# 35 expert tiles a layer in place of 36, and the score banks of each layer's first batch exchanged

## The reference, cut to what matters

```python
x = x + cross_attention(layernorm(x), ctx_1024)        # once, 16 batches of 112 rows of 256
y = layernorm(x)
for l in range(4):                                     # four layers
    y = clip(y + attention(rms(y, ln1_w[l]), wq[l], wk[l], wv[l], wo[l]), -100, 100)
    h = rms(y, ln2_w[l])
    probs = softmax(h @ wr[l]); the two best of 8 experts, their weights made to sum to 1
    y = clip(y + sum over the two experts e of weight * ((silu(h @ wg[l,e]) * (h @ wu[l,e])) @ wd[l,e]), -100, 100)
return x + y
```

## Time and profile before

| | |
|---|---|
| median of 3 runs | 2210.82 us (2205.89 to 2211.4) |
| the profiled execution | 2209.43 us |
| its span, first to last instruction | 2207.6 us |
| mean granted TensorE clock | 0.978 |
| instructions recorded | 34643 |

### The profile page before, as it was taken

The page is one execution under the profiler, slowest core; times in us unless marked ns, Lnnn a source line. Parts: engine busy times, 40 slices in busy tenths (PEclk is TensorE's granted clock), DMA queues, the critical chain, the costliest instruction groups (busy, mean ns, idle before and its releaser), DMA issues.

```text
span 2207.6 us, 34643 instructions
## 1 busy us (share of the span) xinstructions
PE 2062.9 (93%) x9889; PEld 1525.7 (69%) x9890; DVE 1330.2 (60%) x2960; ACT 1033.7 (47%) x3743; POOL 523.4 (24%) x624
## 2 busy tenths in 40 slices
PE   5768999989999999989999999989999999999994
PEld 4646788766667888766667888766667887766663
DVE  4645887764335788754345887744346778844345
ACT  2211667653333766653333667643334676542331
POOL 2212232243012223143011222232011322322023
PEclk9979999999999999999999999999999999999997
DMA  6610233022121232023121222022121331022123
GB/s 187 182 29 34 74 99 103 1 79 84 45 57 52 74 126 71 2 79 89 43 63 44 99 99 70 33 66 76 45 65 35 103 127 39 14 82 69 46 70 94
DMA packets 92023, 157.41 MB, mean 71 GB/s; under 512 B 13874, under 2 KB 65668, under 8 KB 91780
## 3 DMA queue, kind: packets, MB, share of 16 engines
q1 hardware_dynamic: 75988, 114.12, 16.2%
q0 software_dynamic: 15904, 41.64, 6.6%
HBM read 108.75 MB, written 46.97 MB: 71 GB/s over the span
## 4 chain that ended last, share of the span: by engine, by line
PE 62%; DVE 19%; ACT 9%; issue 4%; POOL 3%; DMA 1%; DVEq 0%; SPq 0%; POOLq 0%; ACTq 0%
PE ps L808 23%; PE ps L827 11%; ACT parena L1092 8%; DVE rope L1426 6%; PE ps L707 5%; PE ps L779 5%; PE ps L817 3%; PE ps L728 3%; PE ps L715 2%; PE ps L743 2%; POOL qk L520 2%; DVE rmax L1436 2%; PE ps L682 2%; DVE qk L1414 2%; PE ps L802 1%
## 5 line engine op out<-in xcount | busy, mean ns | idle before, releaser
L808 PE MATMUL ps<-arena,xeT 128*128 x1152 | 544.4, 595 | 5.8 <-ACT xeT L1130 4.5
L1092 ACT ACTIVATE parena<-ps,nmax 112x112 f32<-112x112 f32 x1024 | 345.5, 388 | 120.0 <-DVE nmax L1437 120.0
L808 PEld LDWEIGHTS ps<-arena,xeT 128*128 128x128 f32 x1152 | 209.2, 192 | 151.9 <-issue 144.8
L520 POOL TENSOR_TENSOR qk<-qk,rope 128x448 f32<-128x448 f32 x128 | 148.8, 1163 | 668.0 <-DVE rope L1426 667.8
L1140 ACT ACTIVATE parena<-ps,er 128x512 f32<-128x512 f32 x144 | 99.0, 687 | 405.6 <-PE ps L808 402.0
L707 PE MATMUL ps<-xnT,wqk_s 128*128 128x224 f32 x1280 | 275.7, 359 | 8.9 <-ACT parena L1092 8.0
L487 POOL DMA_INDIRECT y_in<-sorted_y,pos x150 | 143.8, 959 | 554.9 <-DMA sorted_y<-tarena 427.3
L827 PE MATMUL ps<-arena,tarena 128*128 x1152 | 272.6, 379 | 0.8 <-ACT tarena L1146 0.8
L1092 ACT ACTIVATION_READ_ACCUMULATOR parena<-ps,nmax 112x1 f32 x1024 | 246.5, 241 | 0.0
L707 PEld LDWEIGHTS ps<-xnT,wqk_s 128*128 128x128 f32 x1280 | 234.7, 193 | 14.2 <-ACT parena L1092 11.4
L728 PE MATMUL ps<-qk 128*112 128x224 f32 x1024 | 239.5, 356 | 0.0
(11 more groups left out here) (186 smaller groups left out, 2767.6 us busy)
## 6 DMA issues: line engine op xcount, KB each, us to landing
xe<-sorted_x SPq DMA_DIRECT2D x144, 130.0 KB, 2.1
sorted_y<-tarena SPq DMA_DIRECT2D x144, 128.0 KB
arena<-in_L_ffn_wg_dram SPq DMA_DIRECT2D x32, 512.0 KB, 3.6
arena<-in_L_ffn_wu_dram SPq DMA_DIRECT2D x32, 512.0 KB, 4.5
arena<-in_L_ffn_wd_dram SPq DMA_DIRECT2D x32, 512.0 KB, 5.5
arena<-in_ctx_dram SPq DMA_DIRECT2D x16, 375.0 KB
sorted_x<-tarena POOLq DMA_DIRECT2D x8, 585.0 KB, 6.0
sorted_y<-tarena POOLq DMA_DIRECT2D x8, 576.0 KB, 4.9
```

Of the source, the lines that this page charges most:

```text
L520: pool.tensor_tensor(q, q, rope[m % 2][:, :], ALU.add).then_inc(g_rope, 1)
L808: last = pe.matmul(ps[:, bank, :], xeT[u][:, k, :], w[:, bass.ds(e * 1024 + k * 512, 512)], start=(k == 0), stop=(k == KD - 1))
L1092: last = act.activation(prob[:, n, :], ps[0:S, bank, h * S:h * S + S], ACT.Exp, bias=nmax[:, b % 2, n:n + 1], scale=SCALE, accum_out=rsum[ ...
```

## The change

NT becomes 35. TILES holds how many tiles each of the two buffers takes: 18 even and 17 odd. The last tile, 34, is now an even one and uses banks 0 and 1, so batch 0 of each layer has its score halves exchanged: p = 0 in banks 2 and 3, p = 1 in banks 0 and 1 (`score_bank`), and the heads computed during batch 0 move from banks 1 and 2 to 2 and 3. AHEAD stays 26, so that the written out tiles are 26 to 34 in place of 26 to 35. Waits are renumbered to fit. The core of the diff:

```diff
-NT = B * S * TOPK // SLOT + E
+NT = B * S * TOPK // SLOT + E - 1
+TILES = ((NT + 1) // 2, NT // 2)
...
-        ZP = 96
-        zero = tarena[0:ZP, 0:6 * DX].rearrange("p (r d) -> p r d", r=6)
-        rows = ZP * 6
+        ZP = 112
+        zero = tarena[0:ZP, 0:5 * DX].rearrange("p (r d) -> p r d", r=5)
+        rows = ZP * 5
...
-        def heads(p):
+        def score_bank(b, p):
+            return 2 * p if b else 2 - 2 * p
+        def heads(b, p):
+            n = score_bank(b, p)
...
                 with sp.Fori(WHOLE // 2 - 1, NT // 2 - 1) as i:
                     pair(i)
-                if last:
-                    store_rows(0)
-                pair(NT // 2 - 1, end=True)
-                store_tile(NT - 1, 1)
+                load_tile(NT - 1, 0)
+                for T in range(NT - 4, NT):
+                    store_tile(T, T % 2)
+                    if last and T == NT - 3:
+                        store_rows(0)
...
                     if b:
-                        if odd and more:
+                        if odd and more and b > 1:
                             pe.wait_ge(d_rope, l * 40 + (g + 1) * LOADS + 1)
...
-                        heads_of(l, g + 1, 3 if odd else 0, 1)
+                        heads_of(l, g + 1, 3 if odd else 0, 1 if b else 2)
...
-                        heads_of(l, g + 1, 4 if odd else 1, 2)
+                        heads_of(l, g + 1, 4 if odd else 1, 2 if b else 3)
...
-                for i in range(AHEAD // 2, NT // 2):
-                    pair(i, early=not last_layer, end=(i == NT // 2 - 1))
+                for T in range(AHEAD, NT):
+                    tile(T, T % 2, (T + 1) // 2 + 1, early=not last_layer, end=(T == NT - 1))
                 if not last_layer:
                     scores(l + 1, 0, 0)
-                turn_hidden(NT - 1, 1)
+                turn_hidden(NT - 1, 0)
                 if not last_layer:
                     scores(l + 1, 0, 1)
-                down(NT - 1, 1, expert_of(NT - 1))
+                down(NT - 1, 0, expert_of(NT - 1))
...
-            pe.wait_ge(d_rope, 2)
+            pe.wait_ge(d_rope, 4)
             scores(0, 0, 0)
...
-                hidden(NT - 1, 1)
-                copy_result(NT - 2, 0, NT // 2)
+                hidden(NT - 1, 0)
+                copy_result(NT - 2, 1, NT // 2)
                 if not last_layer:
                     maxima(step, l + 1, 0, 0)
                     maxima(step, l + 1, 0, 1)
-                copy_result(NT - 1, 1, NT // 2)
+                copy_result(NT - 1, 0, NT // 2 + 1)
                 if last_layer:
                     for b in range(NT - 2 - AHEAD, B):
                         finish(b)
...
-AHEAD = FIRST + FIRST % 2
-assert AHEAD + 9 == NT - 1 and B - LEAD <= RANK_STEP
+AHEAD = NT - 9
+assert AHEAD > FIRST and AHEAD % 2 == 0
```

More of the change, by code:

```diff
@@ L39 @@
 HROWS = NT * SLOT
-assert NT % 2 == 0 and WHOLE % 2 == 0
+assert NT % 2 == 1 and WHOLE % 2 == 0
 DX = D + 4
@@ L287, in alone @@
             engine.sem_inc(passed, 1)
-        def heads(p):
-            return ps[0:S, 2 * p:2 * p + 2, 0:GN].rearrange("q n (h k) -> q n h k", k=S)
+        def score_bank(b, p):
+            return 2 * p if b else 2 - 2 * p
+        def heads(b, p):
+            n = score_bank(b, p)
+            return ps[0:S, n:n + 2, 0:GN].rearrange("q n (h k) -> q n h k", k=S)
         @block.sync
@@ L401, in layer_io, with pair @@
                     value_weights(l + 1)
-                def pair(i, first=False, end=False, pieces=False):
+                def pair(i, first=False, pieces=False):
                     for u in range(2):
-                        if not end:
-                            load_tile(i * 2 + u + 2, u)
+                        load_tile(i * 2 + u + 2, u)
                         if pieces:
@@ L524, in stored @@
                 for u in range(2):
-                    pool.wait_ge(st_ye[u], l * (8 * NT) + (tiles + 1 - u) // 2 * 16 + 16 - 8 * NT)
+                    pool.wait_ge(st_ye[u], (l - 1) * 16 * TILES[u] + (tiles + 1 - u) // 2 * 16 + 16)
             SOONER = (0, 2, 3, 4)
@@ L725, in scores @@
                 for n in range(2 * p, 2 * p + 2):
-                    pe.matmul(ps[0:S, n, 0:4 * S], ident_b[:, :], bc(causal_b[:, :], 1, [S, 4, S]), start=True, stop=False)
+                    bank = n + score_bank(b, p) - 2 * p
+                    pe.matmul(ps[0:S, bank, 0:4 * S], ident_b[:, :], bc(causal_b[:, :], 1, [S, 4, S]), start=True, stop=False)
                     for i in range(2):
-                        last = pe.matmul(ps[0:S, n, i * 2 * S:(i + 1) * 2 * S], qT[g % 2][:, 2 * n + i, u * S:u * S + S],
+                        last = pe.matmul(ps[0:S, bank, i * 2 * S:(i + 1) * 2 * S], qT[g % 2][:, 2 * n + i, u * S:u * S + S],
                                          keys[g % 2][:, :, p, u * S:u * S + S], start=False, stop=(i == 1))
@@ L797, in turn_tile @@
                 def turn_tile(T, u, n, bank=5):
-                    pe.wait_ge(ld_xe[u], l * (8 * NT) + n * 16)
+                    pe.wait_ge(ld_xe[u], l * 16 * TILES[u] + n * 16)
                     if not (isinstance(T, int) and T == 0):
@@ L945, in tile, with pair @@
                     down(T - 1, 1 - u, expert_of(T - 1))
-                def pair(i, early=False, end=False):
-                    tile(i * 2, 0, i + 1, early=early)
-                    tile(i * 2 + 1, 1, i + 2, early=early, end=end)
+                def pair(i):
+                    tile(i * 2, 0, i + 1)
+                    tile(i * 2 + 1, 1, i + 2)
                 for b in range(B):
@@ L1090, in exponents @@
                 for n in range(8 * p, 8 * p + 8):
-                    bank, h = n // 4, n % 4
+                    bank, h = n // 4 + score_bank(b, p) - 2 * p, n % 4
                     last = act.activation(prob[:, n, :], ps[0:S, bank, h * S:h * S + S], ACT.Exp,
@@ L1162, in iteration @@
                         for u in range(2):
-                            act.wait_ge(st_ye[u], l * (8 * NT) + 16)
+                            act.wait_ge(st_ye[u], l * 16 * TILES[u] + 16)
                     if not odd:
@@ L1435, in maxima @@
                 hs = slice(8 * p, 8 * p + 8)
-                step(dve.tensor_reduce(rmax[:, hs].rearrange("p (n h) -> p n h", n=2), heads(p), AX_X, ALU.max))
+                step(dve.tensor_reduce(rmax[:, hs].rearrange("p (n h) -> p n h", n=2), heads(b, p), AX_X, ALU.max))
                 dve.tensor_scalar(nmax[:, b % 2, hs], rmax[:, hs], -SCALE, None, ALU.mult).then_inc(d_max, 1)
@@ L1615, in layer @@
                         else:
-                            rotate(step, l, g + 1, 0, 1)
+                            rotate(step, l, g + 1, 0, 1 if b else 2)
                     if b:
@@ L1622, in layer @@
                         else:
-                            rotate(step, l, g + 1, 1, 2)
+                            rotate(step, l, g + 1, 1, 2 if b else 3)
                     if b:
@@ L1656, in copy_result @@
                     dve.wait_ge(m_dn, l * NT + T + 1)
-                    dve.wait_ge(st_ye[u], l * (8 * NT) + n * 16)
+                    dve.wait_ge(st_ye[u], l * 16 * TILES[u] + n * 16)
                     dve.tensor_copy(ye[u], ps[:, 6, u * D:u * D + D]).then_inc(m_y, 1)
```

## The result

The changed kernel takes 2186.66 us, the median of 4 runs (2182.84 to 2188.41), against 2209.21 (2205.89 to 2211.4) for the kernel before on the same chip: 22.5 us less, ratio 0.990 with a 95% interval of 0.9888 to 0.9911. The profiled execution took 2187.7 us, its span is 2185.9, 21.7 us shorter than the 2207.6 of the earlier trace rows.

What follows compares the result with a forecast made beforehand. TensorE's queue, without gaps in the expert phase, was taken as the bound. Four tiles of 5.86 us (23.4) less 1.9 us at the end gave 21.5 us, so 2188.5 us was predicted, range 2183 to 2195.

Steps and rivals of the forecast that it cites:

- The tiles: Expert phases: one tile less in each of four layers takes 5.86 us each out of TensorE's chain, 23.4 us.
- the weight loads: Rival for the expert phases: a tile is worth its weight loads, 3.67 us, giving 2197.3 us; chance 0.06.
- The boundary: Between two layers: nothing is late for the next scores, cost 0, bounds 0 and 3 us.
- 4.6 us of cover: Layer boundary: GpSimd's last addition ends at 707.5, 4.6 us before the second half of the scores needs it at 712.1.
- rival (e): Layer boundaries: removed tile was cover for GpSimd's additions, so scores wait; slower from 11.8 us of delay; chance 0.04.
- The exchanged banks: Batch 0's scores and heads: bank exchange counts as nothing; very first maximum 0 to 0.6 us late, taken as 0.
- The end: End of program: finish(7) behind the last copy_result delays gathers 9, 11, 13, 15; 1.9 us given back, bounds 0 and 3.
- The clock: Attention phases: low clock behind batch 13's wait can fall out anew, 3.9 us gain or cost; chance 0.09 each end.
- The bounds of 3.9 us either way: Four attention phases: all at the shortest length would gain 3.9 us, all at the longest would cost 3.9.
- Rows 8: Batch 13, kernel before: instruction behind the 3.39 us wait takes 0.40 us in the first layer, 0.62 in the second.
- the interval named as a sign of being wrong: Attention phases should lie between 264.7 and 266.6 us; one outside would make the prediction wrong.
- The sum: Whole kernel: 23.4 us from tiles less 1.9 at the end, 21.5 us faster, predicted 2188.5 us.

Runs made afterwards that it cites:

- the additional additions: Changed kernel with three or eight idle GpSimd additions ahead of the last rotated addition at each layer boundary: 2186.45 us with three, 2205.36 with eight.

## Why the prediction was right, and where its sizes were off

The time lies 1.8 us below the 2188.5 that was forecast, well in the range, and the forecast mechanism, a full period of TensorE for each tile left out, is what the trace shows.

- **The tiles.** 5.86 us a layer was right to a hundredth. The starts of the products, not the weight loads, were the measure: 3.67 us each would have given 14.7. The rule of the Trainium skill, "Trainium Kernel Development and Optimization", section Performance Expectations, on matmul busy time is about the distance to the roofline; as a price of a removed tile it did not hold here.
- **The boundary.** Nothing was late, as forecast. The 4.6 us of cover were confirmed by the additional additions. What the prediction had wrong is the price behind the cover: "every microsecond ... would be one of TensorE's". The three boundaries paid 3.6, 5.2 and 6.6 us for 3.36 us of idle time each, because the clock can fall behind the wait. In rival (e) the point from which the change loses would come at 8.6 to 11.6 us in place of 11.8; that is an estimate, 4.6 us of cover and the 7.2 us less the 3.2 or 0.2 us that the low clock cost here.
- **The exchanged banks.** Counted at nothing, and worth nothing: without the exchange the time is 2186.73 us. The first maximum of the program waits 0.27 us for TensorE behind the rotations, but the delay is lost, as forecast: batch 0's values start 4.52 us after the last rotation does in both kernels (228.85 to 233.37 before, 229.05 to 233.57 after). The prologue's 0.2 us stand ahead of that.
- **The end.** The mechanism was right, gather 9 behind the last `copy_result`, gather 10 at 4.50 us from it (forecast 4.48). The term was mis-sized: 1.9 forecast, 2.7 measured. Gather 11 was put at 7.61 us behind the `copy_result` and stands at 8.52, because gather 9 landed in 3.57 us in place of the 2.68 that I took from batch 11. The step that failed took one gather's landing for all; the store of finished rows, released by the same `finish(7)`, ran beside this one. The trace of before had such a gather too, number 13 with 3.59 us.
- **The clock.** It was to fall out anew, and did. The attention phases gave 1.2 us back, but not at batch 13. Its wait of 3.4 us was followed by the low clock at once in layers 2 to 4, and before the output projection in the first, which before had none. The largest part given back is at the fourth layer's tile 0, whose wg product ran at 1.2 GHz before and at 2.4 after. The rows are, in order: the last score products and the output projection of batch 13 in the first layer, after; the same output projection, before; wg of tile 0 in the fourth layer, before, then after.

```profile
469.13 1.65 PE L735 MATMUL ps<-qk 128*112 128x224 f32 x4
470.57 4.62 PE L786 MATMUL ps<-wo_s,oT 128*112 128x256 f32 x16
...
469.83 3.62 PE L779 MATMUL ps<-wo_s,oT 128*112 128x256 f32 x16
...
1957.55 3.58 PE L808 MATMUL ps<-arena,xeT 128*128 x4 [1.51 <-ACT xeT L1130]
...
1940.69 1.98 PE L815 MATMUL ps<-arena,xeT 128*128 x4 [1.50 <-ACT xeT L1137]
```

  The bounds of 3.9 us either way were too narrow; that this result kept within them is partly luck. They took the four phases for the same work with the first as the floor. The first phase has a longer start, 13.70 us to batch 0's output projection where the others take 12.39, so the others can come out 1.3 us below it. Rows 8 show only the first instruction behind the wait; in layers 3 and 4 of before the clock fell as well, 0.9 and 0.5 us after that instruction's start. Other executions with the changed kernel's attention went outside the interval named as a sign of being wrong (264.7 to 266.6 us). The rows are the starts of the first two phases in the kernel before, then the second phase of the kernel with the output stores held back and the first phase of the one with batch 7's finish moved.

```profile
233.37:247.07 13.70, 12.30 (x69) 9.48 (x68) 11.35 (x19) 9.14 (x35) 1.89 (x3) 1.00 0.09 15
721.61:734.00 12.39, 12.12 (x69) 9.56 (x68) 10.47 (x17) 8.25 (x31) 1.43 (x2) 1.00 0.03 11
...
716.47:979.64 263.17, 251.85 (x1421) 202.88 (x1420) 201.06 (x412) 174.91 (x730) 78.57 (x80) 1.00 0.21 74
...
230.77:498.64 267.87, 255.38 (x1421) 204.98 (x1420) 201.88 (x413) 176.25 (x736) 77.82 (x81) 0.99 0.23 73
```

  That the gate's measuring runs on freely (the Trainium skill, "TensorE: Matmul & The Clock Gate", Part 1) agrees with this: 3.39 us of idle time in each layer, the low clock at different instructions behind it.
- **The sum.** 23.4 - 1.9 = 21.5 was forecast; 23.4 + 1.2 - 2.7 - 0.2 = 21.7 of span and 22.5 between the medians were measured. Two errors of about a microsecond, the end and the clock, had opposite signs. A part of the 1.8 us is the base: the kernel before had a median of 2210.82 when the forecast was made and 2209.21 with its fourth run.

## What to carry to other kernels

Price a removed piece of work by the distance of the starts in a stretch where the engine never waits; then walk through every item that stood behind the removed piece and set its end against its new deadline. Look also at what merely stood in a loop over the removed piece: here a `finish` slipped behind the last wait and cost 2.7 us of 23.4, and moving one call back made the end 28.4 us again. And before work is moved out of the way of one wait, ask which later wait its own end decides: moving scatters out cost 5.5 us, while moving them forward into a gap of the same queue shortened the wait by the same 2.4 us without a new wait at tile 0; how much of that a whole run keeps is open.

## What the runs showed of the hardware

A gather of 112 rows landed 2.7 us after its second issue alone and 3.6 us with a 448 KB store issued beside it. Behind a wait of 3.4 us on TensorE the granted clock fell at once, a microsecond later or not at all: at the three boundaries with eight additions the same wait cost 0.2, 1.8 and 3.2 us on top of itself. The attention phase, the same work each time, took 263.2 to 266.6 us in layers 2 to 4 of these executions by where the clock fell. In two of the series of executions the same programs took some 60 us longer, with ScalarE standing still for 8 to 10 us at the same place of every layer's expert phase and VectorE beside it.
